# A fused four-block transformer kernel: the order of work in its first stage, and where the first group's loads are issued

## What is computed

```python
x = x + LN(attn(LN(x), q_w, k_w, v_w, out_w, out_b))     # 16 sequences of 512 rows of 128, 16 heads of 8
x = x + LN(ternary_mlp(LN(x), ...))                      # 128 -> 512 -> 512 -> 512 -> 128
x = x + LN(fft_attn(LN(x), w_qkv, w_out))                # cumulative sum over the rows
x = x + LN(mixture(LN(x), ...))                          # a shared expert and one of 8 routed ones
```

## Time and profile before

| | |
|---|---|
| median of 3 runs | 1799.72 us (1798.75 to 1801.79) |
| the profiled execution | 1799.19 us, of which its span is 1797.3 us |
| PE busy | 1580.2 us (88% of the span) |
| DVE busy | 1324.0 us (74%) |
| ACT busy | 1146.9 us (64%) |
| POOL busy | 713.0 us (40%) |

### The profile page before, as it was taken

The page is one execution under the profiler, slowest core; times in us unless marked ns, Lnnn a source line. Parts: engine busy times, 40 slices in busy tenths (PEclk is TensorE's granted clock), DMA queues, the critical chain, the costliest instruction groups (busy, mean ns, idle before and its releaser), DMA issues. The chain is left out here.

```text
span 1797.3 us, 35515 instructions
## 1 busy us (share of the span) xinstructions
PE 1580.2 (88%) x8576; PEld 870.8 (48%) x8577; DVE 1324.0 (74%) x3585; ACT 1146.9 (64%) x2294; POOL 713.0 (40%) x1011
## 2 busy tenths in 40 slices
PE   2899999999999999999499999999498973799996
PEld 1333333333333333333277777777345552566664
DVE  2899999999999999998257666666347763466665
ACT  1387888888888888888466666666236553344342
POOL 2223344344443333322413333333135776144444
PEclk8699999999999999999799999999799985899998
DMA  3333332232323233221010000000120112222210
GB/s 110 75 96 100 86 95 79 81 89 77 93 80 87 79 93 95 72 55 31 13 65 1 1 0 0 0 0 1 27 71 16 44 48 97 72 59 59 59 55 17
DMA packets 84446, 102.48 MB, mean 57 GB/s; under 512 B 15995, under 2 KB 49537, under 8 KB 84368
## 3 DMA queue, kind: packets, MB, share of 16 engines
q1 hardware_dynamic: 78992, 88.89, 17.6%
q0 software_dynamic: 5376, 12.66, 2.0%
HBM read 61.44 MB, written 35.33 MB: 54 GB/s over the span
## 5 line engine op out<-in xcount | busy, mean ns | idle before, releaser
L827 DVE TENSOR_REDUCE bmax<-PS 128x8 f32<-128x512 f32 x1024 | 651.3, 683 | 61.4 <-PE PS L568 58.8
L678 ACT ACTIVATE EX<-PS 128x512 f32<-128x512 f32 x1024 | 565.2, 604 | 107.5 <-PE PS L579 97.9
L568 PE MATMUL PS<-KR,QR 33*128 33x512 f32 x1024 | 411.2, 469 | 50.4 <-DVE bmax L827 31.3
L579 PE MATMUL PS<-QR,KR 64*128 64x512 f32 x1024 | 399.1, 460 | 1.6 <-ACT EX L678 1.5
L568 PEld LDWEIGHTS PS<-KR,QR 33*128 33x128 f32 x1024 | 167.0, 188 | 366.6 <-DVE bmax L827 299.3
L589 PE MATMUL PS<-EX,VS 128*9 128x512 f32 x2048 | 268.6, 596 | 1.2 <-ACT EX L678 1.2
L579 PEld LDWEIGHTS PS<-QR,KR 64*128 64x128 f32 x1024 | 162.5, 185 | 11.3 <-ACT EX L678 10.2
L1024 PE MATMUL PS<-pA,wb 128*128 128x512 f32 x640 | 157.0, 401 | 0.0
L763 POOL TENSOR_TENSOR m_diff<-m_prev,m_all 128x16 f32<-128x16 f32 x64 | 14.2, 222 | 328.1 <-DVE m_all L839 328.1
L1853 ACT ACTIVATE g<-PS 128x512 f32<-128x512 f32 x72 | 43.0, 597 | 142.1 <-PE PS L1813 142.1
L1024 PEld LDWEIGHTS PS<-pA,wb 128*128 128x128 f32 x640 | 120.3, 191 | 27.5
(11 more groups left out here) (227 smaller groups left out, 2821.0 us busy)
## 6 DMA issues: line engine op xcount, KB each, us to landing
QR<-q_scr SPq DMA_DIRECT2D x256, 64.0 KB, 2.4
KR<-k_scr SPq DMA_DIRECT2D x256, 64.0 KB, 2.3
k_scr<-partsB SPq DMA_DIRECT2D x42, 256.0 KB, 2.9
rows<-row_scr SPq DMA_DIRECT2D x72, 129.0 KB, 2.1
q_scr<-partsB SPq DMA_DIRECT2D x28, 256.0 KB, 3.0
X<-in_L_attn_x SPq DMA_DIRECT2D x16, 256.0 KB, 3.0
X<-x SPq DMA_DIRECT2D x16, 256.0 KB, 2.4
xB<-in_L_attn_x SPq DMA_DIRECT2D x14, 256.0 KB, 3.3
```

Source lines behind the costliest of these rows:

```text
L568: pe.matmul(PS[:, bank_of(i, n), :], QR[rows, i, h // 2, t * P:(t + 1) * P], KR[rows, i, h // 2, :], start=True, stop=True).then_inc(tile_ ...
L579: pe.matmul(PS[:, RING3 + bank_of(j, n), :], KR[rows, j, h // 2, kt * P:(kt + 1) * P], QR[rows, j, h // 2, :], start=True, stop=True).then ...
L678: act.activation(EX[:, n % (2 * HG), :], PS[:, RING3 + bank_of(j, n), :], ACT.Exp, scale=SCALE).then_inc(ex_set, 1)
L827: dve.tensor_reduce(bmax[:, i % 2, n, :], PS[:, bank_of(i, n), :].rearrange("p (b k) -> p b k", k=BLK), AX_X, ALU.max).then_inc(tile_max, 1)
```

## The change

It has four parts. In the first block POOL takes the inverse roots of both chunks ahead of the two memsets. PE and ACT finish chunk 0 ahead of chunk 1 (turn 0, project 0, turn 1, project 1). SP issues the eight loads of group 0 in the first block, after chunk 1's stores have been issued, once chunk 0's stores have landed and the memsets are done; only then does it wait for chunk 1's stores. In the second block SP loads chunk 2's X and xB, the output weights and the bias in group 1's step ahead of that group's loads, and not at the block's start; PE and DVE wait for the output weights and the bias where they first use them, in chunk step `b == 2`.

```diff
+        def load_group(sp, b, i):
+            for a in range(2):
+                heads = slice(i * HG + a, (i + 1) * HG, 2)
+                for r in range(2):
+                    rows = slice(HALF * a + r * NPART * HD, HALF * a + (r + 1) * NPART * HD)
+                    sp.dma_start(QR[rows, i].bitcast(F32), q_scr[ds(b, 1), heads]
+                                 .rearrange("b h j d t -> (j d) (b h) t")).then_inc(load_in[i], 16)
+                    sp.dma_start(KR[rows, i].bitcast(F32), k_scr[ds(b, 1), heads, r:r + NPART]
+                                 .rearrange("b h j d t -> (j d) (b h) t")).then_inc(load_in[i], 16)
@@ first block, SP
                 for c in range(AHEAD):
                     store_parts(c, c)
-                for s in range(2):
-                    sp.wait_ge(parts_out[s], PARTS_DMA)
+                sp.wait_ge(parts_out[0], PARTS_DMA)
+                sp.wait_ge(kones, 2)
+                load_group(sp, 0, 0)
+                sp.wait_ge(parts_out[1], PARTS_DMA)
@@ first block, PE
-                run_stages(pe, AHEAD, [(0, turn), (1, project)])
+                turn(0, 0)
+                project(0, 0)
+                turn(1, 1)
+                project(1, 1)
@@ first block, ACT
-                run_stages(act, AHEAD, [(0, copy_xT), (1, cast)])
+                copy_xT(0, 0)
+                cast(0, 0)
+                copy_xT(1, 1)
+                cast(1, 1)
@@ first block, POOL
                 pool.wait_ge(ones_set, 3)
+                for c in range(AHEAD):
+                    rstd(ln1)(pool, c)
 
                 pool.memset(QR[:].bitcast(F32), 0.0).then_inc(kones, 1)
                 pool.memset(KR[:].bitcast(F32), -1.0).then_inc(kones, 1)
-                run_stages(pool, AHEAD, [(0, lambda c, s: rstd(ln1)(pool, c))])
@@ second block, SP
-                sp.dma_start(wo[:], io["L0_attn_out_w"]).then_inc(w3_in, 16)
-                sp.dma_start(bias[:], io["L0_attn_out_b"].to_broadcast([P, P])).then_inc(w3_in, 16)
-                sp.wait_ge(kones, 2)
...
                 def step(b, i, g, has):
-                    if i == 0 and exists(b + 2):
+                    if i == 0 and exists(b + 2) and not (isinstance(b, int) and b == 0):
                         load_x(b)
+                    if isinstance(g, int) and g == 1:
+                        load_x(0)
+                        sp.dma_start(wo[:], io["L0_attn_out_w"]).then_inc(w3_in, 16)
+                        sp.dma_start(bias[:], io["L0_attn_out_b"].to_broadcast([P, P])).then_inc(w3_in, 16)
...
-                        load(b, i)
+                        if not (isinstance(g, int) and g == 0):
+                            load_group(sp, b, i)
@@ second block, PE
-                pe.wait_ge(w3_in, 32)
...
                     elif k == "project":
+                        if isinstance(b, int) and b == 2:
+                            pe.wait_ge(w3_in, 32)
                         by_rows(aT, wo)
@@ second block, DVE
-                dve.wait_ge(w3_in, 32)
...
                 def add_bias(b):
                     dve.wait_ge(use_done, use(b, 0, 3) + 1)
+                    if isinstance(b, int) and b == 2:
+                        dve.wait_ge(w3_in, 32)
```

More of the change, by code:

```diff
@@ L191, in block_kernel @@
         kones = sem("kones")
+        load_in = [sem(f"load_in{i}") for i in range(NG)]
         vs_preset = sem("vs_preset")
+        def load_group(sp, b, i):
[7 more added lines that the diff above has]
+                                 .rearrange("b h j d t -> (j d) (b h) t")).then_inc(load_in[i], 16)
         p1 = ExitStack()
@@ L361, in block_kernel @@
         w_checked = sem("w_checked")
-        load_in = [sem(f"load_in{i}") for i in range(NG)]
         mrow_in = [sem("mrow_in0"), sem("mrow_in1")]
```

## The result

The changed kernel takes 1789.83 us (median of 6 runs, 1788.77 to 1792.38), the kernel before 1799.24 us beside it (6 runs, 1797.83 to 1801.79). The ratio is 0.9948 with a 95% interval of 0.9936 to 0.9960, so 9.4 us come off. The forecast was 1790.0 us.

What follows compares the result with a forecast made beforehand. PE and DVE limit the steady loop, but its start hangs on the chain up to the first score at 46.36 us. Gains of 3.1 + 6.9 less 0.3 make 9.7 us: 1790.0 us, range 1785.0 to 1794.3.

Steps and rivals of the forecast that it cites:

- What bounds it: Chain up to PE's first score at 46.36 us: a microsecond taken from it comes off the end.
- Part 1: First block up to T1: earlier roots and finishing chunk 0 first gain 3.1 us, between 2.3 and 4.0.
- T1: Moment when chunk 1's split ends: 29.50 us before, forecast 26.4, between 25.5 and 27.2.
- a slow and a fast PE: Chunk 1's projection start to T1: 5.93 us at PE's slow pace, 4.26 at its fast pace; the middle taken.
- The inference that single scalings slip in between the memsets: Chunk 1's four scalings on DVE: one or two pass between POOL's memsets, the others wait for the second.
- Part 2: From T1 to the first score: 10.0 us in place of 16.86, gain 6.9, between 5.3 and 7.7.
- The second rival: Loads land no sooner than 4.7 us and DVE waits for xB: gain 6.1, 1793.6; 0.16 with the fourth.
- Part 3: Second block's moved loads and waits: xB lands slightly late for DVE, cost 0.3 us, between 0 and 1.5.
- The first (no hold): Memsets hold nothing, or only until 15.1: T1 at 22.4 or 24.0, gain 12.1 to 13.7, about 1786.8; chance 0.2.
- The slower one: PE's clock in the first groups rises later, 0.24 us lost per microsecond; this or anything taking all the gain 0.04.
- The fourth: First block's end moves into the chain, ending after T1 + 10.0; 3 us more gives 1793; 0.16 with the second.
- The sum: Whole run: 3.1 + 6.9 - 0.3 = 9.7 us gained, execution 1789.5, median of the runs 1790.0.

Runs made afterwards that it cites:

- kernel 4: Changed kernel with one added wait: POOL starts both memsets only after DVE has scaled chunk 1; ratio 0.9927 (0.9914 to 0.9940).
- 7: Changed kernel with POOL's wait for chunk 1's scaling placed between the two memsets; ratio 0.9922 (0.9898 to 0.9945).
- 5: Changed kernel with each of the two memsets cut into 16 pieces; ratio 0.9961 (0.9950 to 0.9973).
- Kernel 2: Changed kernel with POOL's, PE's and ACT's old order in the first block, so only the loads are moved; ratio 0.9960 (0.9944 to 0.9976).
- kernel 1: Kernel before with POOL's edit only, both chunks' inverse roots ahead of the memsets; ratio 1.0006 (0.9996 to 1.0015).
- 6: Kernel before with each of the two memsets cut into 16 pieces; one run, 1800.4 us against a median of 1800.02.
- 8: Changed kernel with X, xB, output weights and bias loaded, and the latter two awaited, at the second block's start as before; ratio 0.9958 (0.9945 to 0.9971).
- kernel 10: Memsets after the scaling, plus 32 unread PE matmuls after chunk 1's projection and 8 at the second block's head; ratio 0.9935 (0.9910 to 0.9960).

## Why the prediction was right, point by point

**What bounds it.** Right. The first score's moment passes to the end of the run: 8.94 us there, 9.3 in the span, 9.4 in the medians; in kernel 4, 13.5 us there and 13.2 by the ratio (0.9927 of 1803). In all twelve rows of the table that have an interval, what the first score gained or lost lies inside it.

**Part 1.** The gain is 2.5 us, forecast 3.1 (2.3 to 4.0). The hold by the memsets was right and is shown by 4 and 7: end of the scaling 19.4 forecast, 19.09 measured. T1 was put at 26.4 as the middle between a slow and a fast PE; PE was slow (6.09 us from the start of chunk 1's projection to T1, 5.93 forecast for that case), and T1 came at 27.03, within the upper end of 27.2. The inference that single scalings slip in between the memsets was wrong (5) and cost nothing, since the end is that of the last memset in either case. The Trainium skill, "SBUF — State Buffer", section "Who interferes with whom", has a VectorE operation in a two-port mode and a GpSimd instruction shut each other out, and leaves one outside these modes with at most one SBUF input alone. The trace agrees: the memsets shut out the scaling (7.52 us in place of 1.11), and the split, with its other input in PSUM, took its usual 1.23 us beside them in kernel 4; in which mode the scaling ran no trace shows. The section lets the one that came first hold on "for the whole instruction"; the runs show more, a hold over all memsets of POOL that follow each other without a wait (7.52 and 8.57 us, against 4.07 with a wait).

**Part 2.** The gain is 6.5 us, forecast 6.9: the eight issues took 3.81 us from first to last and not 3.43 (one into KR took 0.83), and the last landed after 3.3 us and not 3.1. Kernel 2 shows the part alone at 6.5. The second rival's landing of 4.7 did not come: with the loads issued by SP ahead of X and xB the last of them landed after 2.7 to 3.7 us in all nine traces that have them there, with the order of before after 4.6, 6.1 and 5.9 (before, kernels 1 and 6). Against the T1 to first score of these last two the gain would read 7.5 and 7.9 us, so the agreement to 0.4 hangs in part on which execution of before was profiled.

**Part 3.** Forecast 0.3 us lost, measured none: xB landed in 4.3 us (6.0 before). The moved waits were called free; 8 shows that without the move 1.3 to 1.7 us would have been lost. That saving was within the 16.86 us already, so the sum is right.

**The rivals.** The first (no hold) did not happen but can be made, and its price is right: T1 22.4 forecast, 22.08 in kernel 4. The slower one rested on PE's clock; the rise came 29.2 us after the first score, not later than the 32.2 of before. The forecast had it within 1 or 2 us of the same place and at 0.24 us for each; it was 3.1 us sooner and gave 1.2 us, 0.38 for each. Both were put too low. The other traces bear the price out: at the far end, in kernel 1, the rise came 35.8 us after the first score and group 2 took 17.25 us. The fourth needed the first block to end after T1 + 10; it ended at T1 + 7.9.

**The sum.** 2.5 + 6.5 = 9.0 at the first score and 9.4 in the medians, 9.7 forecast. The terms erred by 0.6, 0.4 and -0.3 us, so at the first score the forecast stood 0.8 too high (9.7 against 8.94); the 1.2 us of the clock, which no term held, less the 0.9 lost again later, made up for part of it. That 1790.0 is within 0.2 us of 1789.83 also owes something to the reference, whose median over six runs is 0.5 us below the one that the forecast started from. The mechanism was right in its main parts; the last digit was luck.

## What to carry to other kernels

Where every engine waits for one chain, what the start of the steady loop gains arrives at the end, here within the interval of every ratio. The trace shows where it was gained, which medians of runs that differ by 3 us and more do not. A filler such as a memset, moved off one chain, lands beside something else: ask which operations of the other engines it shuts out and put a wait in front of it, if its result is needed late. Of the parts of an edit, test each alone: here one gained most of it, one gained nothing on its own, and what the third gains alone was left open.

## What the runs showed of the hardware that was not expected

- A run of POOL's memsets without a wait between them holds a 128x128 DVE scaling for as long as the run lasts: 7.52 us with two memsets, 8.57 with 32 pieces, 4.07 with a wait after the first. A 128x4 DVE operation of the same name passes at the next boundary: 2.25 us with whole memsets, 0.29 with pieces. Why it passes stays open. The held one had DVE idle for 1.13 us ahead of it, so it is not that other scalings stood there. The two differ in size, in that the small one takes a constant and the other takes its scale and shift from SBUF, and in what follows them; none of this was tried.
- TensorE fell from 2.4 to 1.2 GHz while at work: in kernel 10 at 36.9 us, after 3 us of scores in which it waited for DVE's reductions between the matmuls, and it stayed there for 27 us (0.50 in the rows from 37 to 64).
- The same eight loads, issued in the same order, landed after at most 4.6 us in the traced execution of the kernel before, and after 6.1 and 5.9 in those of kernels 1 and 6. Issued ahead of X and xB, the last of them landed after 2.7 to 3.7 us in nine traces.
- A held DVE operation is counted as busy for as long as it waits: the first of chunk 1's scalings stands at 6.95 us in place of 0.35. A high busy share of DVE need not be work.
